# A recurrent layer and a mixture of experts: who puts the input product and the recurrent bias into the PSUM banks

## What is computed

```python
x = x + ffn(gru(cond_2048, x, W_ih, W_hh, b_ih, b_hh), Wg, bg, W1, W2)

def cell(h, x):                      # 512 time steps in turn, batch 4, width 512
    gi = x @ W_ih + b_ih             # 512 x 1536
    gh = h @ W_hh + b_hh             # 512 x 1536
    i_r, i_z, i_n = jnp.split(gi, 3, axis=-1)
    h_r, h_z, h_n = jnp.split(gh, 3, axis=-1)
    r = sigmoid(i_r + h_r); z = sigmoid(i_z + h_z)
    n = tanh(i_n + r * h_n)
    return (1.0 - z) * n + z * h

# ffn: 2048 tokens, 4 experts; the two best experts of each token by its logits, softmax over the two,
# each expert takes its best 512 tokens:
#   h = gelu(tok @ W1[i]); out[sel_idx] += h @ W2[i] * p
```

## Time and profile before

| | |
|---|---|
| median of 3 runs (lowest to highest) | 836.67 us (835.92 to 837.12) |
| the profiled execution's own time | 836.27 us |
| its span, first to last instruction | 834.5 us |
| mean granted clock of TensorE in it | 0.987 of full |
| rough steps | from 59 us to 167 us of the span |
| exact steps with fills (20 to 22), then without | from 167 us, from 192 us to 439 us |
| choice of tokens, experts | from 440 us, from 488 us |

### The profile page before, as it was taken

How to read it: one execution, slowest core, us unless ns; L and a number is a source line. 1 busy time by engine, 2 the same in 40 slices (tenths; PEclk the granted TensorE clock), 3 DMA queues, 4 the chain that set the end, 5 groups by cost and what they waited for, 6 DMA issues and landing times.

```text
span 834.5 us, 28320 instructions
## 1 busy us (share of the span) xinstructions
PE 803.0 (96%) x11781; PEld 528.0 (63%) x11782; DVE 619.8 (74%) x2113; ACT 421.1 (50%) x885; POOL 179.9 (22%) x459
## 2 busy tenths in 40 slices
PE   7999999999999999999995799999999999999996
PEld 3446556679999999999994444454445444444442
DVE  6979899878888888888888879767666676755300
ACT  0677666645566556554455448252835184417400
POOL 1002222123433334333330010121012101210011
PEclk9999999999999999999997899999999999999998
DMA  9810000000111010000001943471347224630022
GB/s 336 323 48 2 2 2 3 2 3 4 54 60 50 17 42 5 4 4 5 5 4 33 269 156 119 135 226 27 113 139 194 57 101 151 171 81 1 1 26 26
DMA packets 24286, 62.64 MB, mean 75 GB/s; under 512 B 4386, under 2 KB 4386, under 8 KB 22308
## 3 DMA queue, kind: packets, MB, share of 16 engines
q1 hardware_dynamic: 19312, 51.42, 18.1%
q0 software_dynamic: 3584, 8.42, 5.5%
q10 hardware_dynamic: 1268, 1.08, 0.4%
HBM read 52.50 MB, written 12.62 MB: 78 GB/s over the span
## 4 chain that ended last, share of the span: by engine, by line
PE 92%; DVE 5%; issue 1%; DMA 1%; ACT 0%; POOLq 0%; DVEq 0%
PE ps L459 29%; PE ps L666 20%; PE ps L680 20%; PE ps L451 10%; PE ps L469 3%; PE ps L434 3%; PE ps L424 2%; PE ps L600 1%; PE ps L653 1%; DVE big L1541 1%; PE ps L472 1%; DMA wa<-in_x_t 1%; DVE halves L1264 1%; DVE wa L1253 1%; PE ps L644 0%
## 5 line engine op out<-in xcount | busy, mean ns | idle before, releaser
L459 PE MATMUL ps<-halves,wa 128*128 128x64 f16 x8448 | 289.1, 193 | 1.4 <-DVE halves L1264 1.2
L459 PEld LDWEIGHTS ps<-halves,wa 128*128 128x128 f16 x8448 | 271.2, 98 | 20.2 <-DVE halves L1264 4.2
L680 PE MATMUL ps<-big 128*128 128x512 f16 x768 | 166.9, 379 | 0.0
L666 PE MATMUL ps<-hx,big 128*128 128x512 f16 x768 | 166.9, 379 | 0.0
L779 ACT ACTIVATE wa<-ps,un_gates 128x128 f32<-128x128 f32 x288 | 100.1, 365 | 111.0 <-PE ps L459 100.6
L680 PEld LDWEIGHTS ps<-big 128*128 128x128 f16 x768 | 75.1, 98 | 89.9
L666 PEld LDWEIGHTS ps<-hx,big 128*128 128x128 f16 x768 | 74.8, 98 | 90.0 <-issue 0.2
L784 ACT ACTIVATE wa<-wa,un_gates 128x64 f32<-128x64 f32 x288 | 97.4, 344 | 53.0 <-DVE wa L1253 48.9
L451 PE MATMUL ps<-hx,wb 128*128 128x512 f16 x432 | 106.9, 379 | 1.2 <-issue 1.1
L861 ACT ACTIVATE hx<-ps,un_hid_in 128x512 f32<-128x512 f32 x64 | 43.6, 682 | 109.2 <-PE ps L666 106.9
L1264 DVE SCALAR_TENSOR_TENSOR halves<-ocand,neg_scale,wa 128x64 f16<-128x64 f32 (+1 forms) x288 | 80.6, 280 | 4.4 <-issue 0.5
(11 more groups left out here) (221 smaller groups left out, 791.4 us busy)
## 6 DMA issues: line engine op xcount, KB each, us to landing
wa<-in_w SPq DMA_DIRECT2D x28, 1024.0 KB, 5.2
hs_rows<-big SPq DMA_DIRECT2D x8, 512.0 KB, 6.3
big<-in_w_hh SPq DMA_DIRECT2D x4, 768.0 KB, 19.6
wb<-in_w SPq DMA_DIRECT2D x12, 256.0 KB, 2.6
big<-in_w_ih SPq DMA_DIRECT2D x2, 1024.0 KB, 12.5
hx<-in_x_t SPq DMA_DIRECT2D x2, 1024.0 KB, 16.5
big<-in_w_ih ACTq DMA_DIRECT2D x2, 512.0 KB, 6.6
wa<-in_x_t SPq DMA_DIRECT2D x2, 512.0 KB, 6.2
```

Of the source, the lines that this page charges most:

```text
L459: mm = pe.matmul(gate_ps[:, j, g, :], whh_parts[:, k, w, (4 * g + j) * P:(4 * g + j + 1) * P], halves[:, src, k, h, :], start=False, stop= ...
L666: mm = pe.matmul(ps[:, m % 2, :], w1p[:, w, k, m * P:(m + 1) * P], tokT[:, t, k, :], start=(k == 0 and n == 0), stop=(k == KD - 1 and n == 2))
L680: mm = pe.matmul(ps[:, 2 + g % 2, :], hid[:, h, k, g * P:(g + 1) * P], w2p[:, w, k, :], start=(k == 0 and n == 0), stop=(k == KH - 1 and n ...
```

## The change

The input product for r and z is no longer split: ScalarE's tile goes as fp32 straight to SBUF, laid out by step (r and z of one step side by side). No `diag`, no `split_bhn`, no injects. Each bank is filled ahead of its step instead ("seeded") with the input product times a scale `seed_s` and with `b_hn`, by an engine other than TensorE, and all matmuls of the step add to it.

- For steps 0 to 23 VectorE does it, one pair of instructions for each `j` (128 columns for r and z, 64 for `b_hn`), placed in the step before by `seed_next`.
- For steps 24 to 71 ScalarE does it with four instructions (`seed`): r and z of the three banks j = 0 to 2 at once (384 columns), their `b_hn` at once (192), then the same for j = 3 (128 and 64). The banks j = 0 to 2 exist twice (banks 0 to 2 and 5 to 7) and alternate; bank 3 is single. The call for step i + 1 stands behind `step` of i.
- TensorE waits for the seeds: with `seeded_early` at the first matmul into each bank up to step 23, later with `seeded` at the first matmul of the step (two of the four) and at the first one into j = 3 (all four).
- In rough steps the matmuls are reordered (`ROUGH_ORDER`), and `reset` no longer adds the bias.

The core of the diff:

```diff
-        gate_ps = ps[:, 0:4, 0:3 * COLS].rearrange("p j (g c) -> p j g c", g=3)
+        GATES = 3 * COLS
+        gate_banks = (ps[:, 0:KD - 1, 0:GATES], ps[:, 5:5 + KD - 1, 0:GATES])
+        last_gates = ps[:, KD - 1, 0:GATES]
+
+        def gates_of(bank, j):
+
+            return last_gates if j == KD - 1 else gate_banks[bank][:, j, :]
...
+        ROUGH_ORDER = (((0, 0), (1, 0)), ((0, 1), (1, 1), (2, 0), (2, 1)),
+                       ((3, 0), (3, 1), (0, 2), (1, 2), (2, 2), (3, 2)), ((0, 3), (1, 3), (2, 3), (3, 3)))
...
+        def bank_of(i):
+
+            return int(i >= FILLED and i % 2 == 0)
...
-            def inject(j, c, cols, parts, steps):
-
-                pe.wait_ge(S["rn_done"], steps + j + 1)
-                for part in parts:
-                    pe.matmul(gate_ps[:, j, 0:2, :], diag[:, :], gi_rz[:, c, j, part, :, cols],
-                              start=(part == HIGH), stop=False, skip_group_check=True)
-                if LOW in parts:
-                    pe.matmul(gate_ps[:, j, 2, :], bhn_parts[:, j * P:(j + 1) * P], bhn_unit[:, :], start=False,
-                              stop=False, skip_group_check=True)
...
+                seen = set()
                 for k in range(KD):
                     fill(n + sum(FILLS[:k]), n + sum(FILLS[:k + 1]))
-                    if k == 0 and i % STEPS_C == 0:
-                        pe.wait_ge(S["gi_high"], 8 * (i // STEPS_C) + 8)
                     pe.wait_ge(S["high_ready"], made(i) + k + 1)
-                    for j in range(KD):
-                        if k == 0:
-                            inject(j, *place(i), (HIGH,), KD * i)
-                        unit(HIGH, j, k, src, (HIGH,), k == KD - 1)
-
-            def gates(src, c, cols, base, low_base, steps):
+                    for j, part in ROUGH_ORDER[k]:
+                        if j not in seen:
+                            seen.add(j)
+                            pe.wait_ge(S["seeded_early"], 2 * (KD * i + j + 1))
+                        unit(0, HIGH, j, part, src, (HIGH,), part == KD - 1)
...
+                    if j not in begun:
+                        begun.add(j)
+                        if early:
+                            pe.wait_ge(S["seeded_early"], 2 * (steps + j + 1))
+                        elif j in (ORDER[0][1], KD - 1):
+                            pe.wait_ge(S["seeded"], steps + ((SEEDS if j == KD - 1 else 2) - SEEDS * FILLED))
                     done[j] += 1
-                    unit(h, j, k, src, (HIGH, LOW) if h == HIGH else (HIGH,), done[j] == 2 * KD)
+                    unit(bank, h, j, k, src, (HIGH, LOW) if h == HIGH else (HIGH,), done[j] == 2 * KD)
...
+            def seed(bank, rows_of, before, last_before):
+
+                act.wait_ge(S["rn_done"], before)
+                act.activation(gate_banks[bank][:, :, 0:2 * COLS], rows_of(slice(0, KD - 1)), ACT.Copy,
+                               scale=seed_s[:, 0:1]).then_inc(S["seeded"], 1)
+                act.activation(gate_banks[bank][:, :, 2 * COLS:GATES],
+                               bhn_s[:, 0:KD - 1].unsqueeze(2).to_broadcast([P, KD - 1, COLS]), ACT.Copy
+                               ).then_inc(S["seeded"], 1)
+                act.wait_ge(S["rn_done"], last_before)
+                act.activation(last_gates[:, 0:2 * COLS], rows_of(KD - 1), ACT.Copy, scale=seed_s[:, 0:1]
+                               ).then_inc(S["seeded"], 1)
+                act.activation(last_gates[:, 2 * COLS:GATES], bhn_s[:, KD - 1:KD].to_broadcast([P, COLS]), ACT.Copy
+                               ).then_inc(S["seeded"], 1)
+
+            def seed_ahead(i):
+
+                if i == FILLED:
+                    act.wait_ge(S["gi_kept"], 12 * NC_)
+                    act.wait_ge(S["seeds_known"], 1)
+                c = (i // STEPS_C + CHUNK_ORDER[0]) % NC_
+                seed(bank_of(i), lambda j: gi_rz[:, c, j, i % STEPS_C, :], KD * i, KD * (i + 1))
...
-                step(KD * i)
+                step(KD * i, bank_of(i))
+                if FILLED <= i + 1 < FIRST + L and i >= FILLED:
+                    seed_ahead(i + 1)
...
+                if i + 1 == FILLED:
+                    seed_ahead(FILLED)
...
-            def rz_high(t):
-
-                c, m = TILES[t]
-                dve.wait_ge(S["gi_kept"], t + 1)
-                dve.tensor_copy(gi_rz[:, c, m % 4, HIGH, m // 4, :], gi_full[:, rz_count(t) % GI_RING, :]
-                                ).then_inc(S["gi_high"], 1)
-
-            def rz_low(t):
-
-                c, m = TILES[t]
-                dve.wait_ge(S["gi_high"], rz_count(t + 1))
-                dve.tensor_tensor(gi_rz[:, c, m % 4, LOW, m // 4, :], gi_full[:, rz_count(t) % GI_RING, :],
-                                  gi_rz[:, c, m % 4, HIGH, m // 4, :], ALU.subtract).then_inc(S["gi_low"], 1)
...
+            def seed(i, j):
+
+                c = (i // STEPS_C + CHUNK_ORDER[0]) % NC_
+                dve.tensor_scalar(gates_of(0, j)[:, 0:2 * COLS], gi_rz[:, c, j, i % STEPS_C, :], seed_s[:, 0:1], None,
+                                  ALU.mult).then_inc(S["seeded_early"], 1)
+                dve.tensor_copy(gates_of(0, j)[:, 2 * COLS:GATES], bhn_s[:, j:j + 1].to_broadcast([P, COLS])
+                                ).then_inc(S["seeded_early"], 1)
+
+            dve.wait_ge(S["gi_kept"], 12)
+            for j in range(KD):
+                seed(0, j)
...
+                def seed_next(j):
+
+                    if following is None:
+                        return
+                    if j == 0 and following % STEPS_C == 0:
+                        dve.wait_ge(S["gi_kept"], 12 * (following // STEPS_C + 1))
+                    seed(following, j)
...
+                         (one_less_z, 0), (candidate_in, 2), (blend, 0), (seed_next, 0), (keep_state, 0), (one_less_z, 1),
+                         (reset, 3), (blend, 1), (seed_next, 1), (candidate_in, 3), (one_less_z, 2), (keep_state, 1),
+                         (blend, 2), (seed_next, 2), (one_less_z, 3), (keep_state, 2), (blend, 3), (seed_next, 3),
+                         (keep_state, 3), (low_part, 2), (low_part, 3))
+                rough = ((reset, 0), (candidate_in, 0), (reset, 1), (candidate_in, 1), (seed_next, 0), (one_less_z, 0),
+                         (reset, 2), (blend, 0), (candidate_in, 2), (seed_next, 1), (one_less_z, 1), (reset, 3), (blend, 1),
+                         (candidate_in, 3), (seed_next, 2), (one_less_z, 2), (blend, 2), (seed_next, 3), (one_less_z, 3),
+                         (blend, 3), (other_work, 0))
```

More of the change, by code:

```diff
@@ L710, in _ @@
             act.wait_ge(S["tables"], 1)
-            act.wait_ge(S["bhn_clear"], 1)
-            for row in ROW_OF:
-                act.dma_start(bhn_row[row:row + 1, :], b_hn).then_inc(S["bhn_loaded"], 16)
             act.wait_ge(S["bias_ready"], 1)
@@ L766, in _ @@
                 x_high(0, k)
-            for m in range(3, ACT_HIGHS):
+            for m in range(3, TILES_EARLY):
                 first_tile(m)
-                first_tile_high(m)
             act.wait_ge(S["gates_known"], 1)
@@ L1228, in w1_peak, with step @@
                 dve.tensor_reduce(peak[:, W1:W1 + 1], sq[:, :], AX.X, ALU.max).then_inc(S["w_peak"], 1)
-            def step(gi_n, after, src, base, low, moved=False, ahead=(), between=(), bias_added=True):
+            def step(gi_n, after, src, base, low, bank, moved=False, between=(), following=None):
                 dst = 1 - src
@@ L1337, in _ @@
                     after = lambda j, i=i: hs[:, j, i - FIRST + 1, :]
-                ahead, between = [], []
-                if i < FILLED:
-                    for t in range(split_by(i - 1), split_by(i)):
-                        if TILES[t][1] < 8:
-                            (ahead if s == STEPS_C - 1 else between).append((rz_high, t))
-                            (ahead if i == FILLED - 1 else between).append((rz_low, t))
+                between = []
                 if 1 <= s <= KD and q < 2:
```

160 lines of the change are left out of this document (49 added, 111 removed).

## The result

| | before | after |
|---|---|---|
| median | 836.81 us | 953.01 us (946.39 to 959.51, 4 runs) |
| ratio | | 1.139, interval 1.131 to 1.147 |
| span of the profiled execution | 834.5 us | 951.2 us |
| mean granted clock | 0.987 | 0.970 |

The change makes the kernel 14% slower, 116 us. The forecast was 928, its range 905 to 985.

What follows compares the result with a forecast made beforehand. TensorE's streams were taken to bound the kernel. Terms of 86.5 + 5 + 2.0 + 0.5 - 1.7 - 1.1 = +91.2 us on 836.3 gave 927.5, or 928 us on the median's footing; range 905 to 985.

Steps and rivals of the forecast that it cites:

- The change in the steps 25 to 71: Exact steps: TensorE waits 2.39 us for seeds behind tanh 3, step 6.84 us against 5.00, +86.5 us in all.
- The clock: Steps 25 to 71: TensorE's pauses let its clock fall to half three times in 47 steps, +5 us.
- the second rival: Exact steps: the clock falls in most steps, 1003 us, or in half of them, 963 us; chance 17%.
- Rough steps: The 20 rough steps: four VectorE seed pairs of 0.36 us against TensorE's saved injects, put at 0 us.
- what TensorE saves, the blend takes: Rough steps: about 0.22 us saved on TensorE is used up by a last blend about 1.25 us later, net 0.
- Steps 20 to 24, and ahead: Steps 20 to 22 -1.7 us, step 23 +2.0, step 24 +0.5; ahead of the steps -1.1.
- The sum: Whole kernel: all terms add up to +91.2 us, 927.5, and 928 us on the median's footing.
- the forecast's own case: Whole kernel: the forecast without its rivals, 928 us, between 905 and 950; chance 72%.
- Rival 1: Exact steps: seeds come in time, step 4.68 us, 15 us less in all, 821 us; chance 3%.
- What bounds the kernel now: Exact steps before the change: TensorE's 0.26 + 4.45 us, with 0.29 of injects, make up the 5.00 us step.

Runs made afterwards that it cites:

- Run 1: The changed kernel with ScalarE's first pair of seeds for step i + 1 ahead of sig 0 of step i, not behind tanh 3: 848.67 us, ratio 1.014.
- run 4: The changed kernel with VectorE's seed pairs behind the blends in rough steps and all bank 3 products in the last group: 934.58 us.
- Run 2: The changed kernel with 36 unread products of ones in each exact step from 25 on, ahead of the wait for the seeds: 932.99 us.
- run 3: The changed kernel with all products into bank 3 moved into the last group of the rough steps: 944.94 us.
- run 8: The kernel before with 8 of 12 inject products per exact step left out: 1080.92 us with a further round; steps 24 to 71 took 235.90 us (before 236.05).
- run 5: The changed kernel with the order changes of Run 1 and run 4 together: 840.59 us, ratio 1.0045.

## Why the prediction was right, and where it was off

- *The change in the steps 25 to 71.* Right in mechanism and size. The wait was 2.41 against 2.39, its parts 1.20, 0.26, 0.50, and 0.45 for the second seed with the way to the product, against 1.21, 0.25, 0.51 and 0.42; the 144 products and sig 3 took 4.40 against 4.45; the step 6.81 against 6.84. Run 1 shows that the place of the seeds is the cause. The estimates of the unseen writes into PSUM held, by the groups of the profile after (busy us, mean ns):

```profile
L750 ACT ACTIVATE ps<-big,seed_s 128x384 f32<-128x384 f32 x48 | 27.1, 566 | 0.0
L756 ACT ACTIVATE ps<-big,seed_s 128x128 f32<-128x128 f32 x48 | 16.9, 351 | 0.0
L752 ACT ACTIVATE ps<-bhn_s 128x192 f32<-128x192 f32 x48 | 14.9, 311 | 0.0
L758 ACT ACTIVATE ps<-bhn_s 128x64 f32<-128x64 f32 x48 | 9.8, 204 | 0.0
```

  566 for an estimate of 610 and 311 for 360. The first is far above its low bound (0.50 from start to start, the bound was 0.27), the second a little under its own (0.34). The rule of the Trainium skill that stood beside them ("ScalarE: Activation LUTs", "Step-by-step: what each stage is for") points the right way here, by about 45 ns an instruction, 4 us over the 47 steps; no run writes the same columns to SBUF, so that PSUM is the reason is not shown.
- *The clock.* The term that was mis-sized most: three falls and 5 us taken, 11 falls found in the profiled execution, 4 in the same steps of run 4. Run 2 measures the term: 20.2 us. The price of one, 1.75, was about right (1.84), in part by luck: the earlier trace rows show 3.8 us of work at half pace and not 3.5 (450 to 452, and 1.8 of the next two), and that fall lasts 10.2 us in the trace (443.6 to 453.8), where those of the kernel after last 3.4. The number of falls was a guess between none and the second rival's "most steps". The rival's rule, that of the Trainium skill in "TensorE: Matmul & The Clock Gate", section "HAM oscillation — how this bites in real kernels", came true in a quarter of the steps. Falls at 289.2 and 296.0, at 326.8 and 333.6, at 371.2 and 378.0 and at 528.4 and 535.2 come in pairs one step apart; why these steps and not others I can't say. Since their number differs between executions, so does the time (946 to 960).
- *Rough steps.* The step "what TensorE saves, the blend takes" failed: 0 taken, +0.54 a step measured, within the bounds of -0.2 to +1.2. The pair cost what was put, 0.38 against 0.36:

```profile
L1168 DVE TENSOR_SCALAR ps<-big,seed_s 128x128 f32<-128x128 f32 x96 | 33.2, 346 | 3.3 <-ACT big L723 3.1
L1170 DVE COPY ps<-bhn_s 128x64 f32<-128x64 f32 x96 | 20.8, 216 | 0.0
```

  The last blend ends 5.39 behind sig 0 instead of 3.96 (it ended at 92.78, sig 0 at 88.82), 1.43 later instead of 1.25. And I looked at the last blend alone. The order of TensorE, which the front part of this text shows, opens bank 3 in the third group, and its wait for the fourth pair cost 5.2 of the 10.9 us (run 3). An added wait has to be followed on the engine that waits, not only on the one that is waited for.
- *Steps 20 to 24, and ahead.* +1.0 against +0.8, and -1.8 against -1.1.
- *The sum.* The measured time is 25 us above the 928: 15 are the clock and 11 the rough steps, both counted too low, and the 47 waits took 2.5 less than put. 953 is inside the range, but above the 950 that the forecast's own case allowed; the room up to 985 was there for the second rival. (The low end adds up to 907, 928 less 12, 5 and 4, and not to 905.)
- *Rival 1.* Its price was wrong. With the seeds in time (run 1) the step is 4.99, not 4.68. I had closed the loop by blend 0 and the 81 products behind it, and left out that the last of the 81 need low part 3. The same slip stands in "What bounds the kernel now": 0.26 + 4.45, and 0.29 of injects, add up to 5.00, but the 0.29 was no proof. In run 8 most of these injects were gone and the step stayed. A sum that closes doesn't show that its terms are on the path.

No version beat the kernel before; the best, run 5, is 0.45% behind. The change takes work off an engine that didn't bind the exact steps, and puts it on two whose order did.

## What to carry to other kernels

Work that is moved from one engine to another gets the place in the other's queue, and it is this place that has a price: the same instructions cost 106 us behind the last tanh and nothing measurable ahead of the first sigmoid. Before taking work off the busiest engine, close the loop of dependencies by every operand of the last product, and test whether it binds by leaving some of its work out: 96% busy did not mean bound. And a new pause in a steady stream of matmuls costs twice, by its length and by the clock that may fall behind it.
